# Modulation blocks in nine places, all asked for at once, and pieces spread over the end of each pass

## What is computed

```python
mod = (_silu(c) @ wmod).reshape(1, 6, 1, -1)          # c: 1 x 1024, wmod: 1024 x 6144
sa, ca, ga, sb, cb, gb = (mod[:, i] for i in range(6))
ga = (2 * (ga >= 0) - 1) * jnp.maximum(jnp.abs(ga), 0.25)   # gb the same
h = _layernorm(x) * (1 + ca) + sa
# selective scan, 16 states for each of the 1024 channels
xp = h @ x_proj_w.T                                    # 32 columns for dt, 16 for B, 16 for C
dt = softplus(xp[:, :32] @ dt_proj_w.T + dt_proj_b)
state_t = exp(dt_t * A) * state_{t-1} + dt_t * B_t * h_t;  y_t = sum(state_t * C_t) + D * h_t
x = x + ga * y
h = _layernorm(x) * (1 + cb) + sb
gate, up = h @ gate_w.T + (h @ gate_a.T) @ gate_b.T, the same for up     # 2752 columns each
hidden = silu(gate) * up
x = x + gb * (hidden @ down_w.T + (hidden @ down_a.T) @ down_b.T)
```

## Time and profile before

| | |
|---|---|
| median of 3 runs | 2260.53 us (2260.38 to 2260.57) |
| the profiled execution | 2265.11 us |
| its span, first to last instruction | 2263.3 us |
| TensorE / VectorE / ScalarE / GpSimd busy | 2026.9 / 1441.1 / 1044.8 / 1558.3 us |
| mean granted TensorE clock | 0.945 of full |
| bytes moved by DMA | 594.13 MB, 263 GB/s over the span |

### The profile page before, as it was taken

The page is one execution under the profiler, slowest core; times in us unless marked ns, Lnnn a source line. Parts: engine busy times, 40 slices in busy tenths (PEclk is TensorE's granted clock), DMA queues, the critical chain, the costliest instruction groups (busy, mean ns, idle before and its releaser), DMA issues.

```text
span 2263.3 us, 32653 instructions
## 1 busy us (share of the span) xinstructions
PE 2026.9 (90%) x11470; PEld 1836.5 (81%) x11470; DVE 1441.1 (64%) x2118; ACT 1044.8 (46%) x2337; POOL 1558.3 (69%) x968
## 2 busy tenths in 40 slices
PE   6597748888778889899999999999999999999999
PEld 3243227777768889899899889899889999999999
DVE  5676776778666778766778766778767774211111
ACT  3777765666453555444554443554444332210000
POOL 4679879999977877977877876877869886110100
PEclk8798768989999999999999999999999999999999
DMA  9799966778767677576667576667577877787786
GB/s 351 273 363 392 340 242 247 264 283 298 273 244 260 212 269 266 207 284 222 217 233 267 186 282 228 217 234 267 186 266 252 284 247 270 244 297 266 258 292 215
DMA packets 120051, 594.13 MB, mean 263 GB/s; under 512 B 10448, under 2 KB 22992, under 8 KB 80208
## 3 DMA queue, kind: packets, MB, share of 16 engines
q1 hardware_dynamic: 119888, 592.04, 73.4%
HBM read 506.97 MB, written 85.03 MB: 262 GB/s over the span
## 4 chain that ended last, share of the span: by engine, by line
PE 58%; DVE 17%; ACT 8%; POOL 7%; issue 7%; DMA 2%; DVEq 0%; ACTq 0%; SPq 0%; POOLq 0%
PE FP L852 48%; DVE ring L1277 7%; DVE ring L1165 3%; PE FP L735 3%; POOL ring L1414 3%; DVE FP L1252 2%; ACT SC L931 2%; POOL y L1373 2%; PE FP L877 1%; PE FP L813 1%; PE FP L769 1%; POOL xlo L1405 1%; DMA wts<-w_scratch 1%; DMA modw<-mod_w 1%; DVE hb L1237 1%
## 5 line engine op out<-in xcount | busy, mean ns | idle before, releaser
L852 PE MATMUL FP<-xhi,wts 128*128 128x368 f32 (+2 forms) x4224 | 1055.1, 326 | 72.2 <-ACT dtb L1060 20.9
L852 PEld LDWEIGHTS FP<-xhi,wts 128*128 128x128 f32 x4224 | 757.3, 194 | 81.1 <-issue 69.9
L1414 POOL TENSOR_TENSOR ring<-ring,c_row 128x736 f32<-128x736 f32 (+2 forms) x336 | 575.0, 1712 | 252.5 <-ACT hst L948 252.4
L852 PE MATMUL FP<-xlo,wts 128*128 128x368 f32 (+2 forms) x2112 | 685.0, 324 | 0.0
L931 ACT ACTIVATE SC<-dtb,aneg 128x368 f32<-128x368 f32 (+2 forms) x768 | 409.7, 539 | 574.5 <-DVE ring L1277 573.9
L852 PE MATMUL FP<-hhi,wts 128*128 128x368 f32 (+5 forms) x2376 | 572.6, 322 | 14.2 <-POOL hlo L1430 4.4
L1277 DVE TENSOR_TENSOR_SCAN ring<-SC,hst,ring 128x368 f32<-128x368 f32 (+1 forms) x640 | 579.9, 948 | 4.2 <-ACT SC L931 3.8
L1373 POOL TENSOR_TENSOR y<-y,ring 128x736 f32<-128x736 f32 (+1 forms) x320 | 555.6, 1736 | 13.9
L852 PEld LDWEIGHTS FP<-hhi,wts 128*128 128x128 f32 (+1 forms) x2376 | 408.5, 186 | 22.6 <-issue 10.0
L852 PEld LDWEIGHTS FP<-xlo,wts 128*128 128x128 f32 x2112 | 409.6, 194 | 1.1
L852 PE MATMUL FP<-hlo,wts 128*128 128x368 f32 (+5 forms) x1188 | 379.5, 319 | 0.0
(11 more groups left out here) (119 smaller groups left out, 2008.0 us busy)
## 6 DMA issues: line engine op xcount, KB each, us to landing
wts<-w_scratch SPq DMA_DIRECT2D x243, 1152.0 KB, 5.2
wts<-w_scratch SPq DMA_DIRECT2D x91, 896.0 KB, 4.9
wts<-w_scratch SPq DMA_DIRECT2D x51, 1024.0 KB, 5.8
w_scratch<-wts SPq DMA_DIRECT2D x43, 1152.0 KB, 8.2
modw<-mod_w SPq DMA_DIRECT2D x24, 1024.0 KB, 10.5
raw<-w_gu SPq DMA_DIRECT2D x29, 576.0 KB, 8.4
w_scratch<-wts SPq DMA_DIRECT2D x16, 896.0 KB, 8.6
w_scratch<-wts SPq DMA_DIRECT2D x9, 1024.0 KB, 6.0
```

The costliest lines, as they stand in the source:

```text
L852: last = mm(out, w, x, start=(start and k == 0 and e == 0), stop=(stop and k == n - 1 and e == 2))
L1414: G.tensor_tensor(buf, buf, over_pair(c_of(k)), ALU.mult).then_inc(g_hc, 1)
```

## The change

- **Places.** Blocks 0 to 4 keep the slots of `modw`; 5, 6, 7 and 11 go to tiles that are not in use yet (`y1`, `y2`, `ring`, `hb1`). Blocks 8, 9 and 10 follow 0, 1 and 2. SP asks for all twelve blocks of ca, sa and ga, and for four weight units, ahead of any piece; x_proj comes behind block 7 and dt_proj behind block 8, each with its own semaphore.
- **Who makes which block.** VectorE 0, 3, 5, 8, 10; GpSimd 1, 4, 9; TensorE 2, 6, 7, 11 and on.
- **Scale and shift by pairs.** sa is copied in three parts (blocks 4 and 5, block 6, block 7), and `aff` of chunk 0 waits for its pair of tiles; `proj` waits for a pair at a time, in every chunk. 1 + ca is made by the copy itself.
- **Step size ahead of the gate.** `soft` ends with dt; u is a piece of its own, `u`, behind it, and `keep` waits for dt instead of u. In the start, `soft` and `keep` of tiles 0 and 1 go ahead of ga's finish, which reads the columns from PSUM.
- **Preps 0 and 1** go from the start to either side of `first`.
- **Pass ends.** The pieces of units 63 and 64 stay with their units; on TensorE they come behind that unit's "begin", on VectorE ahead of `used` of the unit before.

The diff, cut to its core:

```diff
-BY_VECTOR = [0, 3, 5, 10, 9]
-BY_GPSIMD = [1, 4]
-BY_TENSOR = [2, 7, 6, 8] + list(range(MOD_FIRST + 1, MOD_BLOCKS))
-LATES = [range(MOD_EACH * n, MOD_EACH * (n + 1)) for n in range(3)] + [range(b, b + 1) for b in range(3 * MOD_EACH, MOD_BLOCKS)]
+BY_VECTOR = [0, 3, 5, 8, 10]
+BY_GPSIMD = [1, 4, 9]
+BY_TENSOR = [2, 6, 7] + list(range(11, MOD_BLOCKS))
+LATES = [range(0, 4), range(4, 6), range(6, 7), range(7, 8), range(8, 12)] + [range(b, b + 1) for b in range(12, MOD_BLOCKS)]
+GATE_LATE = 4
+MOD_HOMES = {5: "y1", 6: "y2", 7: "ring", 8: "hb1"}
 
 
 def mod_slot(b):
-    return b % MOD_SLOTS if b < MOD_FIRST else (b - MOD_FIRST) % MOD_LATE
+    if b < 8:
+        return b
+    return 8 if b == 11 else (b - 8) % MOD_LATE if b < 11 else (b - 12) % MOD_LATE
...
-    for k, kind in enumerate(("dt", "sp", "soft", "keep")):
-        HEAD_AT.setdefault(33 + 3 * i + k, []).append((kind, i))
+    for k, kind in enumerate(("dt", "sp", "soft", "u", "keep")):
+        HEAD_AT.setdefault(33 + 3 * i + k - (k > 2), []).append((kind, i))
...
-    out = vrow(0) + [("vcopy", 0)] + grow(1) + [("sum", 0, 0), ("sum2", 0, 0)] + cen(0, 0) + row(2) + [("rowc", 2), ("sq", 0, 0), ("sq2", 0, 0)]
-    out += vrow(3) + [("vcopy", 3), ("lprep",)] + grow(4) + vrow(5) + [("vcopy", 5), ("rstd", 0, 0), ("consts",), ("col", 0), ("col", 1), ("col", 2), ("col", 3), ("late", 0)]
-    out += row(7) + [("rowc", 7)] + [("norm", 0, 0, q) for q in range(PAIRS)] + prep() + row(6) + [("rowc", 6), ("col", 4), ("col", 5), ("col", 6), ("col", 7)]
-    out += [("late", 1), ("mod", 0)] + prep() + [("aff", 0, 0, q) for q in range(PAIRS)] + row(8) + [("rowc", 8)] + vrow(10) + [("vcopy", 10)] + vrow(9) + [("vcopy", 9)]
-    out += [("proj", 0), ("xs", 0), ("lx", 1), ("dt", 0, 0), ("dt", 0, 1)] + row(11) + [("sp", 0, 0), ("rowc", 11)]
-    out += [("col", 8), ("col", 9), ("col", 10), ("col", 11), ("late", 2), ("mod", 1)]
-    out += [("ini", 0, 0), ("soft", 0, 0), ("sp", 0, 1), ("keep", 0, 0), ("soft", 0, 1), ("keep", 0, 1), ("first",)]
+    out = [("vrow", 0), ("vcopy", 0), ("grow", 1), ("sum", 0, 0), ("sum2", 0, 0)] + cen(0, 0) + row(2) + [("rowc", 2), ("sq", 0, 0), ("sq2", 0, 0)]
+    out += [("vrow", 3), ("vcopy", 3), ("grow", 4)] + cols(0, 1, 2, 3) + [("vrow", 5), ("rstd", 0, 0), ("late", 0), ("vcopy", 5), ("consts",)]
+    out += [("norm", 0, 0, q) for q in range(PAIRS)] + row(6) + [("rowc", 6)] + cols(4, 5) + [("late", 1), ("aff", 0, 0, 0), ("aff", 0, 0, 1)]
+    out += row(7) + [("rowc", 7)] + cols(6) + [("late", 2), ("aff", 0, 0, 2)] + cols(7) + [("late", 3), ("aff", 0, 0, 3), ("dtw",)]
+    out += [("vrow", 8), ("vcopy", 8), ("grow", 9), ("vrow", 10), ("proj", 0), ("xs", 0), ("vcopy", 10), ("lx", 1), ("dt", 0, 0), ("dt", 0, 1)]
+    out += row(11) + [("sp", 0, 0), ("rowc", 11), ("sp", 0, 1)] + cols(8, 9, 10, 11) + [("soft", 0, 0), ("keep", 0, 0), ("soft", 0, 1), ("keep", 0, 1)]
+    out += [("late", 4), ("mod", 1), ("ini", 0, 0), ("u", 0, 0), ("u", 0, 1)] + prep() + [("first",)] + prep()
...
+LATE_PIECES = [LAST_LORA + 1, LAST_LORA + 2]
...
-    for u in (LAST_LORA + 1, LAST_LORA + 2):
-        at[LAST_LORA] += at[u]
-        at[u] = []
...
-            for b in range(MOD_SLOTS):
+            for b in range(3):
                 load_mod(b)
             sp.dma_start(vec[:, 0, :], dt_bias).then_inc(d_const, 16)
             sp.dma_start(vec[:, 1, :], d_vec).then_inc(d_const, 16)
             sp.dma_start(aneg[:, :], a_log).then_inc(d_const, 16)
             sp.dma_start(eye[:, :], ident).then_inc(d_const, 16)
-            sp.dma_start(xpw[:, :, :], x_proj).then_inc(d_const, 16)
-            sp.dma_start(dtw, dt_proj).then_inc(d_const, 16)
+            for b in range(3, 8):
+                load_mod(b)
+            sp.dma_start(xpw[:, :, :], x_proj).then_inc(d_xpw, 16)
+            load_mod(8)
+            sp.dma_start(dtw, dt_proj).then_inc(d_dtw, 16)
+            for b in range(9, 12):
+                load_mod(b)
+            for i in range(PREP_BUFFERS):
+                load_prep(next(k for k in range(NPREP) if raw_of_prep(k) == i))
...
-                    pe.wait_ge(a_h, PAIRS * (c + 1))
                     if c == 0:
-                        pe.wait_ge(d_const, N_CONST)
-                        pe.wait_ge(a_const, 4)
-                        pe.wait_ge(g_const, 1)
+                        pe.wait_ge(d_xpw, 16)
                     bank_free(pe, *p)
                     for i in range(ND):
+                        if i % 2 == 0:
+                            pe.wait_ge(a_h, PAIRS * c + i // 2 + 1)
...
+                    if u in LATE_PIECES:
+                        unit(c, u, "begin")
                     for p in PIECES[c][u]:
                         piece(p)
-                    if u == LAST_LORA:
-                        for v, step in ((u, "begin"), (u + 1, "begin"), (u, "end"), (u + 2, "begin"), (u + 1, "end"), (u + 2, "end")):
-                            unit(c, v, step)
-                    elif u not in (LAST_LORA + 1, LAST_LORA + 2):
+                    if u in (LAST_LORA, *LATE_PIECES):
+                        unit(c, u if u == LAST_LORA else u - 1, "begin" if u == LAST_LORA else "end")
+                        if u == LATE_PIECES[-1]:
+                            unit(c, u, "end")
+                    else:
                         unit(c, u)
...
-                        if c == 0 and q == 0:
-                            act.wait_ge(v_mod, 1)
+                        if c == 0:
+                            act.wait_ge(v_late, max(2, q + 1))
...
-                    act.wait_ge(v_u, t + 1)
+                    act.wait_ge(v_add, t + 1)
...
+                if n == 1:
+                    dve.wait_ge(pe_col, LATES[GATE_LATE][-1] + 1)
+                    V.scalar_tensor_tensor(out=mod[:, GA, :], **signed(FP[:, at, 0:ND])).then_inc(v_late, 1)
+                    dve.wait_ge(v_late, GATE_LATE + 1)
                     V.tensor_tensor(gad[:, :], mod[:, GA, :], vec[:, 1, :], ALU.mult).then_inc(v_mod, 1)
                 else:
...
-                    if g and last != "gate":
+                    if g and last != "gate" and u not in LATE_PIECES:
                         used(*divmod(g - 1, NU))
-                    if UNITS[u][:2] == ("down", len(PARTS) - 1) and UNITS[u][2] == 0:
-                        lora_low(c)
                     for p in PIECES[c][u]:
                         piece(p)
+                    if u in LATE_PIECES:
+                        used(*divmod(g - 1, NU))
+                    if u == LATE_PIECES[0]:
+                        lora_low(c)
             used(CHUNKS - 1, NU - 1)
```

More of the change, by code:

```diff
@@ L344, in bank_plan @@
         for u in range(NU):
-            order += PIECES[c][u] + [("unit", c, u)]
+            order += [("unit", c, u)] + PIECES[c][u] if u in LATE_PIECES else PIECES[c][u] + [("unit", c, u)]
     place = {item: i for i, item in enumerate(order)}
@@ L355, in free_at @@
             return place[("cen" if kind == "sum" else "norm", *item[1:], PAIRS - 1)]
-        return place[{"proj": ("xs", *item[1:]), "dt": ("keep", *item[1:]), "vrow": ("vcopy", item[1]), "row": ("rowc", *item[1:]), "col": ("late", late_of(item[1]))}[kind]]
+        if kind == "proj":
+            return place["xs", item[1]]
+        if kind == "dt":
+            return max(place["u", item[1], item[2]], place["keep", item[1], item[2]])
+        if kind == "vrow":
+            return place["vcopy", item[1]]
+        if kind == "row":
+            return place["rowc", item[1]]
+        return place["mod", 1] if late_of(item[1]) == GATE_LATE else place["late", late_of(item[1])]
     bank, before, last = {}, {}, [None] * BANKS
@@ L429, in build @@
         d_const, d_c = sem("const_loaded"), sem("c_loaded")
+        d_xpw, d_dtw = sem("xproj_loaded"), sem("dt_weights_loaded")
         d_x = [sem(f"x_loaded{s}") for s in range(3)]
         d_out = [sem(f"out_stored{s}") for s in range(3)]
[L432 removed]
+        d_mod = [sem(f"mod_loaded{s}") for s in range(MOD_SLOTS + len(MOD_HOMES))]
         d_prep = [sem(f"prep_loaded{s}") for s in range(PREP_BUFFERS)]
@@ L493, in bank_free @@
                 engine.wait_ge(a_keep, ND * user[1] + user[2] + 1)
+                engine.wait_ge(v_u, ND * user[1] + user[2] + 1)
             elif kind == "vrow":
@@ L665, in _ @@
                     load_x(p[1])
-                elif p[0] == "lraw":
-                    load_prep(next(i for i in range(NPREP) if raw_of_prep(i) == p[1]))
-                elif p[0] == "lprep":
-                    for i in range(RAW_SLOTS):
-                        load_prep(i)
                 elif p[0] == "prep":
@@ L727, in mod_cols @@
                     elif b in BY_GPSIMD:
-                        last = mm(out, gacc[:, BY_GPSIMD.index(b), i * P:(i + 1) * P], ones[:, 0:1], start=True, stop=True)
+                        last = mm(out, gacc[:, BY_GPSIMD.index(b) % 2, i * P:(i + 1) * P], ones[:, 0:1], start=True, stop=True)
                     else:
@@ L940, in copy_c @@
```

(20 more changed lines are left out.)

97 lines of the change are left out of this document (54 added, 43 removed).

## The result

The changed kernel takes 2242.06 us (median of 4 runs, 2236.83 to 2242.7) against 2260.55 of the kernel before in the same rounds: the ratio is 0.9908, with a 95% interval of 0.9891 to 0.9925. The profiled execution took 2242.7, 0.6 above the median; that of before was 4.6 above its own, so the spans (2263.3 and 2240.8) lie 22.5 apart, 4 more than the medians.

The account below looks back on a forecast made before the run. TensorE was taken to bound the passes, a chain of waits the start, nothing full in the scan. Span 2263.3 - 9 (start) - 4.5 (ends) = 2249.8; 2251.6 for an execution, less 4.6: 2247 us, range 2236 to 2256.

Parts of the forecast that it names:

- Start: Before the scan's first product: the start gets 9 us shorter, between 7 and 12.
- asking for all at once: Block loads in the start: all requested together, block n lands at 11.6 + 2.5n, plus 0.4 for constants behind block 2.
- DMA: Scan of chunk 0: the 4.4 MB moved into it fit at 369 GB/s against 350, so no cost was taken.
- The sign that was named for a cost: In the scan: if ScalarE waits for weight loads, DMA gave the start's gain back.
- The rival that DMA gives the start back: In the scan: 6.3 us come back, giving 2253, or 2260 at all of the upper bound; chance 0.17.
- The Trainium skill's limit: In the scan: at near 358 GB/s of HBM per core, 84 MB take 235 us, 7 more than the stretch has.
- Pass ends: Ends of passes 0 to 3: 4.5 us gained, bounds 1 and 16; 2.5 in pass 0, 1 each in passes 1 to 3.
- Clock up everywhere: TensorE keeps 2.4 GHz through the new waits: 26 us gained in all, 2235; chance 0.13.
- Slower by both waits: Pass ends: squares stay late and TensorE pays old and new waits, 22 us in four passes, 2273.5; chance 0.12.
- The signs of being wrong: Row 11 or block 9 later than 54, a longer scan to first pass, or pass ends moving over 3 us each.

Follow-up runs that it names:

- start_only: The changed kernel with its pass ends bunched at unit 62 again, as in the kernel before; 2252.44 us against 2262.17, ratio 0.9958.
- q_aff_whole: sq_before_begin with chunk 0's scale and shift waiting for all four shift blocks instead of going by pairs; first product at 60.65, ratio within 0.9839 to 0.9851.
- q_loads_wait: sq_before_begin with blocks 5, 6 and 7 asked for only when blocks 0, 1 and 2 have been used; ratio 0.9851.
- ends_only: The kernel before with only the pass ends spread over units 62 to 64; 2253.91 us against 2262.17, ratio 0.996.
- extra_copies: The changed kernel with four unused DRAM-to-DRAM copies of a modulation block (4.2 MB in all) added in chunk 0's scan; 2244.76 us, ratio 0.9924.
- sq_before_begin: The changed kernel with the first half of the sum of squares moved back ahead of unit 62's "begin"; 2227.14 us, ratio 0.9843.
- q_warm: sq_before_begin with TensorE repeating the eight matmuls of `proj` once in its wait for `xs`; ratio 0.9849.

## Why the prediction was right, step by step

- **Start, 9 forecast: 9.5** by the first product (62.63 for 72.14) and 9.5 by start_only's ratio. The closeness is in part luck. The forecast had 10.2 at the first product (61.9) and took 1.3 off for prep 1 behind `first`; measured were 9.5 there, and no part of the 1.3, since the scan up to the first pass was as long as before (277.2 for 277.1). The order was also as told: block 5 at 24.04 (24.6), then the late VectorE blocks and not `aff` set `xs`, then row 11 sets the second `sp`. `aff` was 1.7 later than forecast, because row 6 ran at the low clock behind a wait of 1.42 us; q_aff_whole shows that this much is hidden. `xs` ended 1.4 later (47.3 for 45.9), since block 8 began at 38.63, behind the last shift column, and not at 37.1. Row 11 ended at 54.1 for 52.8. Softplus and the gate's tail took less than I gave them, and the sum came out within 0.7.
- **What was argued but not the cause:** the gain of the blocks was put down to asking for all at once, although the prediction itself saw that SP wasn't late. By q_loads_wait the waits that fell away are worth 1 us or so; the rest of the blocks' gain is, by exclusion, their order in the queue and on TensorE. The step size first is worth 2.0 of the 9.5.
- **DMA, 0 forecast: 0 in the length of the scan.** The scan moved 370 GB/s where 369 were worked out, and from first product to first pass it took 277.2 against 277.1. In other executions, of kernels from either side, it took 273.2 to 275.3 (273.4 in ends_only, 273.2 in q_aff_whole), so a cost of up to 4 us can't be excluded from single profiles; start_only's 9.5 us by the times is the start's whole gain, but its interval (5.9 to 12.9) is no narrower. The sign that was named for a cost did show a little: ScalarE waited 3.3 us in all (4.1 in start_only) for DMA in this stretch, and not at all in before and ends_only. It waited for stores and not for loads, and lost no time by it that the stretch shows. The rival that DMA gives the start back fell, but extra_copies shows how near it was.
- **The Trainium skill's limit** (DMA: Bandwidth & Descriptors, Specifications: about 358 GB/s of HBM per core) would have made the scan 7 us longer, by the prediction's estimate. The scan ran at 370 and with the copies at 380 GB/s, so for this core working alone the limit doesn't hold. The Trainium skill, same page, section Measured, has 425 GB/s for a single core in a transfer of 16 MB that GpSimd issued. These rows, of transfers that SP issued, stay below that, the blocks' 416 too.
- **Pass ends, 4.5 forecast (1 to 16): 7.5** by the table (221.5 to 214.0), 9 by ends_only's ratio. The mechanism was right, wait by wait; the sizes were off. The term took 1 us for each of passes 1 to 3, on the ground that the clock falls in the new wait as it did in the old. In the kernel after it fell in passes 1 and 2, which gained 1.2 and 0.9 as forecast, and not in pass 3, which gained 4.9. In ends_only it fell in passes 1 and 3 (-0.5 and 3.4) and not in pass 2 (4.0), in extra_copies in passes 2 and 3 (0.9 and 3.4) and not in pass 1 (3.3). So it fell in six of nine cases, and where it stayed up the gain was 3.3 to 4.9: a term of 1 with a chance of two in three and 4 with one in three would have been nearer. The fall, taken at 2.65 us, cost 1.5 in pass 2 (8.60 for 7.08) and at most 2.6 (pass 1 of ends_only: 8.8 from the wait to the squares, where extra_copies took 6.2). Pass 0, given 2.5, gained 0.4: its wait for the low part is 4.85 long, not 2.9, and the trace of before had this, as TensorE began the squares at 619.23 and the low part ended at 624.08.
- **The other rivals.** Clock up everywhere (2235): it came true in part of the passes only. Slower by both waits (2273): no wait for the squares was left in any pass, in the kernel after or in ends_only.
- **The signs of being wrong.** One was touched: row 11 ended at 54.13, where 54 was the limit. The pass ends were not to move by over 3 us each; one of the four did, that of pass 3, by 4.9. The scan was 0.1 longer from first product to first pass, which is no difference.
- **The rest of the 22.5 us** between the two profiles, some 5.6 in passes 1 and 3 outside their ends, is absent in ends_only as a sum (-0.6). The profile of before was itself 4.6 above its median, after's 0.6, and that may be most of it, but it isn't shown. Pass 3 outside its end took 284.2 in before, 283.6 in start_only and 287.5 in ends_only, but 282.7 in after, 281.0 in extra_copies and 280.7 in sq_before_begin, which all have both halves. A wait of TensorE at the head of the pass goes the same way: 2.4, 2.5 and 4.0, then 1.5 and none in the last two. Whether the two halves together bring this or chance does is open.

## What to carry to other kernels

When a wait is bared by moving work behind it, look for a piece that is ready and split it: 2.6 us of squares ahead of the wait and the rest behind it gave more than twice what the move alone had given (18.3 us over four pass ends, against 7.5, in the profiles). Look at what stands ahead of a late load in its queue before looking for more room for it. A wait of TensorE can be paid twice, once in idle time and once in the clock behind it, so filling it can be worth more than the time of the wait: in q_warm useless matmuls in a wait of 5.2 us brought what stood behind it 2.2 us forward, though the first product's gain of that size is below what the times can tell here.
